# Random-feature attention: the norms placed in the spare rows of the projection's operand, one product for two, and the end of the chain moved a step

## The reference, cut to what matters

```
def _feature_map(x, rf):
    proj = jnp.einsum('bhnd,fd->bhnf', x, rf) / jnp.sqrt(jnp.float32(NUM_FEATURES))
    norm = jnp.linalg.norm(x, axis=-1, keepdims=True)
    return jnp.exp(proj - norm)
# on layernorm(x):  q' = feature_map(q), k' = feature_map(k)
kv = einsum('bhnf,bhnd->bhfd', k', v)
normalizer = einsum('bhnf,bhf->bhn', q', k'.sum(axis=2))
out = einsum('bhnf,bhfd->bhnd', q', kv) / (normalizer + 1e-06)
y = out @ w_out.T + b_out
x1 = x + layernorm(y);  what goes to the next layers is layernorm(x1)
```

## Time and profile before

| | us |
|---|---|
| median of 3 runs | 1756.01 |
| lowest and highest | 1754.92, 1756.5 |
| the profiled execution's own time | 1755.7 |
| its span | 1753.9 |
| PE busy | 1674.9 (95%) |
| DVE busy | 1446.5 (82%) |
| ACT busy | 1299.2 (74%) |
| POOL busy | 1039.0 (59%) |

### The profile page before, as it was taken

How to read it: one execution, slowest core, us unless ns; L and a number is a source line. 1 busy time by engine, 2 the same in 40 slices (tenths; PEclk the granted TensorE clock), 3 DMA queues, 4 the chain that set the end, 5 groups by cost and what they waited for, 6 DMA issues and landing times. The chain is left out here.

```text
span 1753.9 us, 54573 instructions
## 1 busy us (share of the span) xinstructions
PE 1674.9 (95%) x18245; PEld 1154.1 (66%) x18373; DVE 1446.5 (82%) x3283; ACT 1299.2 (74%) x3588; POOL 1039.0 (59%) x1015
## 2 busy tenths in 40 slices
PE   6999999979999999999989997999999999998997
PEld 4666666646777777777765664777777777775664
DVE  3777777769999999999967776899999999986996
ACT  5888888848998998989982224998998998985221
POOL 1333333337777777777763324777777777775664
PEclk9999999989999999999999999999999999999999
DMA  3211111111111111111113321111111111113443
GB/s 118 69 48 48 48 48 48 43 43 35 44 39 39 42 40 37 42 42 36 42 50 94 92 76 37 38 43 45 33 42 45 33 42 45 33 40 88 110 122 86
DMA packets 201095, 94.02 MB, mean 54 GB/s; under 512 B 82578, under 2 KB 192060, under 8 KB 201020
## 3 DMA queue, kind: packets, MB, share of 16 engines
q1 hardware_dynamic: 201020, 93.06, 20.1%
HBM read 51.00 MB, written 25.23 MB: 43 GB/s over the span
## 5 line engine op out<-in xcount | busy, mean ns | idle before, releaser
L846 ACT ACTIVATE pr<-banks,nb,rr 128x128 f32<-128x128 f32 x1024 | 456.3, 465 | 5.0 <-DVE nb L915 5.0
L747 POOL TENSOR_TENSOR rr<-ss,half_neg 128x16 f32<-128x16 f32 x128 | 374.4, 2925 | 19.0 <-POOL ss L744 17.0
L764 POOL TENSOR_TENSOR pr<-pr,rl 128x512 f32<-128x512 f32 x256 | 266.5, 1041 | 103.3 <-DVE rl L877 103.3
L885 DVE TENSOR_REDUCE ss<-sq 128x16 f32<-128x1024 f32 x128 | 156.1, 1219 | 75.4 <-ACT sq L795 61.3
L846 ACT ACTIVATION_READ_ACCUMULATOR pr<-banks,nb,rr 128x1 f32 x1024 | 216.5, 211 | 0.0
L1216 ACT ACTIVATE f_g<-banks,b_s 128x512 f32<-128x512 f32 (+1 forms) x96 | 65.9, 686 | 202.0 <-PE banks L1300 192.2
L893 DVE TENSOR_REDUCE mx<-banks 128x8 f32<-128x1024 f32 x128 | 156.0, 1219 | 9.0 <-PE banks L1022 8.3
L383 POOL TENSOR_SCALAR a_ve<-a_mv 128x2 f32<-128x2 f32 x96 | 21.4, 223 | 226.5 <-DVE a_mv L394 223.4
L755 POOL TENSOR_TENSOR krot<-ka,rr 128x512 f32<-128x512 f32 x128 | 134.4, 1050 | 22.3 <-POOL rr L747 11.7
L974 PE MATMUL banks<-ident,pr 128*128 128x128 f32 x1024 | 141.2, 281 | 5.9 <-POOL pr L764 5.9
L837 ACT COPY pT<-banks 128x512 f32<-128x512 f32 x128 | 75.1, 587 | 95.9 <-PE banks L974 95.9
(11 more groups left out here) (126 smaller groups left out, 4210.4 us busy)
## 6 DMA issues: line engine op xcount, KB each, us to landing
ve<-vt SPq DMA_DIRECT2D x128, 128.0 KB, 2.2
hs<-y_d SPq DMA_DIRECT2D x128, 64.0 KB, 2.0
yt<-y_d SPq DMA_DIRECT2D x64, 128.0 KB, 2.1
y_d<-yn SPq DMA_DIRECT2D x64, 128.0 KB, 2.0
f_h<-y_d SPq DMA_DIRECT2D x128, 64.0 KB, 2.0
f_y<-y_d SPq DMA_DIRECT2D x64, 128.0 KB, 2.2
xa<-in_L_attn_x SPq DMA_DIRECT2D x32, 128.0 KB, 2.2
xr<-in_L_attn_x SPq DMA_DIRECT2D x32, 128.0 KB, 2.3
```

The costliest lines, as they stand in the source:

```text
L747: nc.gpsimd.tensor_tensor(rr[:, r, :], ss[:, r, :], half_neg[:], ALU.pow).then_inc(T["rr"], 1)
L764: nc.gpsimd.tensor_tensor(pr[:, e], pr[:, e], rl[:, e].unsqueeze(2).broadcast_to([P, UH, P]), ALU.mult).then_inc(T[("ne", "no")[e]], 1)
L846: a = nc.scalar.activation(pr[:, e, j, :], bank[e][:, j * P:(j + 1) * P], ACT.Exp, bias=nb[:, X.t, UH * e + j:UH * e + j + 1], scale=rr[:, ...
L885: nc.vector.tensor_reduce(ss[:, 2 * X.p + X.t, :], sq[:].rearrange("p (h d) -> p h d", d=DH), AX.X, ALU.add).then_inc(T["ss"], 1)
```

## The change

The row of a head's norm moves. In each group of 32 rows the heads 0 and 1 own the rows 0 to 15, the heads 2 and 3 the rows 16 to 31; now the norms of heads 0 and 1 are put in rows 16 and 17 and those of heads 2 and 3 in rows 0 and 1. For each pair of heads one operand of 32 rows is built, which holds the pair's data in its own half and its norms in the other, and one product with `rfx` = `rfa` + `rfn` replaces the two. GpSimd multiplies the copied q and k by a column of ones and zeros, once for each pair (`qkm`), and VectorE adds the norms, multiplied by the opposite column (`xn2`). The q features need as many columns as before in one product in place of two (16 products become 8); the k features need 16 products as before, of 128 columns instead of 256. PE's product of k features and values now stands ahead of the sums of squares. The normalisation of y, x1, its statistics, its inverse deviation, its store and `a_yo` are done one step later, and `a_yo` on GpSimd.

```
 norm_rows:
-            row = 32 * g + h
+            row = 32 * g + (16 + h if h < 2 else h - 2)
+    lower = (np.arange(P) % 32 < 16).astype(np.float32)
+    return neg, np.concatenate([ones, own, np.stack([lower, 1.0 - lower], 1)], 1)
 setup_vector:
+            dve.wait_ge(set_done, 2 + 1 + 5)
+            nc.vector.tensor_tensor(rfx[:], rfa[:], rfn[:], ALU.add).then_inc(set_done, 1)
 a_sync:
             if on.last:
                 n = i - 3
+                sp.wait_ge(A["x1"], n + 1)
+                sp.dma_start(x1_d[...], a_x1[:, 1 - p]).then_inc(A[f"out{1 - p}"], 16)
                 sp.wait_ge(A["yo"], n + 1)
                 ...
-            if on.tail:   (the same store, n = i - 2)
 a_pool:
+            if on.now:
+                pool.wait_ge(A["sq"], i + 1)
+                until(pool, A["xn2"], 2 * i)
+                apart(pool)
+                for a in range(2):
+                    j = nc.gpsimd.tensor_scalar(qkm[:, a], qkT[:], hones[:, P + 4 + a:P + 5 + a], None, ALU.mult)
+                j.then_inc(A["qkm"], 1)
+            if on.last and part in (None, 1):
+                (wait yn, xr_in, out)
+                nc.gpsimd.tensor_tensor(a_x1[:, 1 - p], a_y2[:], xr[:, 1 - p], ALU.add).then_inc(A["x1"], 1)
             if on.tail: inv_std of y, i - 2
+            if on.last: inv_std of x1, i - 3
             if on.pre: inv_std of the input
+            if on.last and part in (None, 2):
+                pool.wait_ge(A["rs3"], n + 1)
+                apart(pool)
+                for t in range(TPB):
+                    j = nc.gpsimd.tensor_scalar(a_yo[:, 1 - p, t, :], a_x1[:, 1 - p, t, :], a_mv3[:, t, 0:1],
+                                                a_rs3[:, t:t + 1], ALU.subtract, ALU.mult)
+                j.then_inc(A["yo"], 1)
 a_act:
+                until(act, A["qkm"], i)        (ahead of the copy into qkT)
+                until(act, A["xn2"], 2 * i)    (ahead of the square root)
 a_pe, behind, q features:
-                    for w, src in ((rfa, qkT), (rfn, nrm)):
-                        for c in range(4):
-                            m = matmul(bank[c][:, a * N:(a + 1) * N], w[r, a * P:(a + 1) * P],
-                                       src[r, 1 - p, 0, :], start=w is rfa, stop=w is rfn)
+                    for c in range(4):
+                        m = matmul(bank[c][:, a * N:(a + 1) * N], rfx[r, a * P:(a + 1) * P],
+                                   xn2[r, 1 - p, a, 0, :], start=True, stop=True)
 a_pe, order after it: product of k features and values, sums of squares, output projection,
   transposition of the product, v projection, transposition of the input
 a_pe, now, k features:
-                pe.wait_ge(A["nrm"], i + 1)
-                for t in range(TPB):
-                    for w, src in ((rfa, qkT), (rfn, nrm)):
-                        for c in range(4):
-                            m = matmul(bank[c][:, t * N:(t + 1) * N], src[r, p, 1, t * P:(t + 1) * P],
-                                       w[r, :], start=w is rfa, stop=w is rfn)
+                for a in range(2):
+                    pe.wait_ge(A["xn2"], 2 * i + a + 1)
+                    for t in range(TPB):
+                        for c in range(4):
+                            m = matmul(bank[c][:, t * N + a * P:t * N + (a + 1) * P],
+                                       xn2[r, p, a, 1, t * P:(t + 1) * P], rfx[r, a * P:(a + 1) * P],
+                                       start=True, stop=True)
 a_dve, order after the input normalisation (a_yo is gone): normalisation of y of i - 3, copy of the
   product, bias of y of i - 2, placing in kvb, and then
+            if on.now:
+                dve.wait_ge(A["nrm"], i + 1)
+                dve.wait_ge(A["qkm"], i + 1)
+                until(dve, A["qf_ps"], i - 1)
+                for a in range(2):
+                    nc.vector.scalar_tensor_tensor(out=xn2[:, p, a].rearrange("p q n -> p (q n)"), in0=nrm[:],
+                                                   scalar=hones[:, P + 5 - a:P + 6 - a], in1=qkm[:, a],
+                                                   op0=ALU.mult, op1=ALU.add).then_inc(A["xn2"], 1)
   and the statistics of y (i - 2), of x1 (i - 3) and of the input (i + 2)
 between the stages:
   SP: the steps B+1 and B+2 of a_sync stand in slots 3 and 5 of stage T (before: 1 and 3)
   POOL, DVE: the step B+2 stands in the slots 2 and 3, in two parts (before: DVE alone, in slot 3)
```

More of the change, by code:

```diff
@@ L472, in a_act @@
                 nc.scalar.activation(a_sq[:], bank[4][:], ACT.Square)
-                nc.scalar.copy(qkT[:, p].rearrange("p a n -> p (a n)"), bank[4][:]).then_inc(A["sq"], 1)
+                until(act, A["qkm"], i)
+                nc.scalar.copy(qkT[:], bank[4][:]).then_inc(A["sq"], 1)
             if on.behind:
@@ L481, in a_act @@
                 act.wait_ge(A["ss_ps"], i + 1)
-                nc.scalar.activation(nrm[:, p].rearrange("p a n -> p (a n)"), bank[4][:], ACT.Sqrt
-                                     ).then_inc(A["nrm"], 1)
+                until(act, A["xn2"], 2 * i)
+                nc.scalar.activation(nrm[:], bank[4][:], ACT.Sqrt).then_inc(A["nrm"], 1)
                 act.wait_ge(A["v_ps"], i + 1)
@@ L545, in a_pe @@
             if on.now:
+                pe.wait_ge(A["sq"], i + 1)
+                nc.tensor.matmul(bank[4][:], hones[:, 0:P], a_sq[:], start=True, stop=True).then_inc(A["ss_ps"], 1)
+            if on.tail:
+                pe.wait_ge(A["o"], k + 1)
+                for t in range(TPB):
+                    m = nc.tensor.matmul(bank[7][:, t * P:(t + 1) * P], a_oT[:, t * P:(t + 1) * P],
+                                         wT[:, 3, :], start=True, stop=True)
+                m.then_inc(A["w_ps"], 1)
+            if on.behind:
+                pe.wait_ge(A["kvT"], n + 1)
+                for r in range(2):
+                    m = nc.tensor.transpose(bank[5][:, N + r * P:N + (r + 1) * P], a_kvT[:, r * P:(r + 1) * P],
+                                            ident[:])
+                m.then_inc(A["kv_ps"], 1)
+            if on.now:
                 if on.tail:
@@ L626, in a_dve @@
                 nc.vector.tensor_copy(a_kvT[:], bank[5][:, 0:N]).then_inc(A["kvT"], 1)
+            if on.tail and part in (None, 1):
+                dve.wait_ge(A["w_ps"], k + 1)
+                if on.last:
+                    dve.wait_ge(A["yn"], l + 1)
+                nc.vector.tensor_tensor(a_y[:], bank[7][:, 0:N].rearrange("p (t d) -> p t d", d=D),
+                                        bout[:].unsqueeze(1).broadcast_to([P, TPB, D]), ALU.add).then_inc(A["y"], 1)
+            if on.behind:
                 dve.wait_ge(A["kv_ps"], n + 1)
@@ L636, in a_dve @@
                 j.then_inc(A["kv"], 1)
-            if on.tail and part in (None, 2):
-                dve.wait_ge(A["rs2"], k + 1)
-                until(dve, A["x1"], k)
-                for t in range(TPB):
-                    j = normal(a_y2, a_y, a_mv2, a_rs2, t)
-                j.then_inc(A["yn"], 1)
+            if on.now:
+                dve.wait_ge(A["nrm"], i + 1)
[5 more added lines that the diff above has]
+                                                   op0=ALU.mult, op1=ALU.add).then_inc(A["xn2"], 1)
+            if on.tail and part in (None, 1):
+                dve.wait_ge(A["y"], k + 1)
+                until(dve, A["rs2"], k)
+                stats(dve, a_y, a_st2, a_mv2, TPB, A["st2"], 2 * (k + 1), A["mv2"])
+            if on.last and part in (None, 2):
+                dve.wait_ge(A["x1"], l + 1)
+                until(dve, A["yo"], l)
+                stats(dve, a_x1[:, 1 - p], a_st3, a_mv3, TPB, A["st3"], 2 * (l + 1), A["mv3"])
             if on.pre:
```

85 lines of the change are left out of this document (31 added, 54 removed), and 2 rows, old and new, of the table A.

## The result

The changed kernel takes 1757.64 us (median of 20 runs, 1755.09 to 1762.26), the kernel before 1755.10 (20 runs, 1753.33 to 1758.39): the ratio is 1.0016, with an interval of 1.0010 to 1.0022. The forecast was 1749.7 us and faster. The measurement says no change, or 0.1 to 0.2% slower.

The account below looks back on a forecast made before the run. PE's work, nearly level with a ring through ACT, was taken as the bound. 31 steps x (10.7 - 10.96 + 0.01) = -7.8, +1.5 at the ends, from 1755.7: 1749.4, as median 1749.7 us; range 1731 to 1766.

Parts of the forecast that it names:

- The step: One looped step of stage A, first product to next first product: from 10.96 us to 10.67, taken as 10.7 with waits.
- T: In stage A, the start of a step's first product on PE, from which the prediction counts its times.
- I take 0.80: GpSimd's mask, a `tensor_scalar` of 128x512 in stage A: 0.80 us each, between estimates of 0.77 and 1.04.
- 0.36 a half: `a_yo` on GpSimd: 0.36 us for each half, 0.7 in all.
- So the first half of `a_xn` waits for mask A, the second for mask B: VectorE in stage A takes whole-instruction turns with GpSimd's masks; without that a step would be 10.05 us.
- Rival (1): GpSimd's masks become stage A's bound: 1763 us with masks of 1.04, 1777 with 1.27; chance 0.30.
- G: Length of one GpSimd mask in stage A, forecast 0.80 us; a step was put at 9.07 + 2G.
- Rival (2): Stage A's masks and `a_xn` don't hinder each other, or masks are under 0.5: step 10.05, total 1729 us; chance 0.20.
- Rival (3): Stage A's k features stay bound by operand loads at 1.94 us: step 11.07, total 1761 us; chance 0.10.
- PE idle 1 to 2 us ahead of the k features: A sign in stage A that the forecast is right: PE idles 1 to 2 us, ended by `xn2`.
- Sum at the ends +1.5 (0 to +4): Filling and draining of stage A, including stage T's later start, together cost 1.5 us, between 0 and 4.
- I work out 0.7 later: At stage T's start, SP's `hs` loads wait for `a_yo` of batch 29 on GpSimd: 0.7 us later.

Follow-up runs that it names:

- e2: The changed kernel with GpSimd's two masks as a product of two tensors, the second a broadcast column, instead of `tensor_scalar`: 1779.13 us, ratio 1.0144 to the kernel before.
- e5: The changed kernel with the chain's end as before (`a_yo` on VectorE, y's statistics ahead of the product's copy), one product kept: 1808.17 us, ratio 1.0298.
- e9: e7 plus one wait, so that GpSimd starts x1 only when the pair `xn2` is done: 1736.76 us, ratio 0.9900 to the kernel before.
- e1: The changed kernel with two filler products on PE ahead of its wait for `xn2`: 1752.39 us, ratio 0.9990 to the kernel before.
- e8: e6 with the masks taken from GpSimd, one made by ACT's scaled copy, the other by VectorE from bank 4: 1760.99 us, ratio 1.0035 to the kernel before.
- e10: e9 without the two filler products: 1742.54 us, ratio 0.9921 to the kernel before.
- e4: The kernel before with only the chain's end moved a step later and `a_yo` on GpSimd, no masks, two products for the features: 1761.64 us, ratio 1.0043.
- e7: e6 with the `a_yo` of the last two batches on VectorE in slots 3 and 4 of stage T: 1742.14 us, ratio 0.9925 to the kernel before.
- e3: The changed kernel with SP's first `hs` loads for stage T issued ahead of its wait for `a_yo` of batch 29: 1750.27 us, ratio 0.9978 to the kernel before.
- e6: The changed kernel with both the filler of e1 and the early loads of e3: 1746.35 us, ratio 0.9948 to the kernel before.
- e11: e9 with the second half of `a_yo` left out in the looped steps, so output incomplete: 1734.06 us (one run).

## Why the prediction was wrong

**The step was right, by errors that cancel.** Forecast 10.67, measured 10.65; that the two agree is luck. The placing ends 0.52 earlier than forecast, and the pair takes 0.42 longer. Counted from T = 209.55 as in the prediction:

| | forecast | measured |
|---|---|---|
| q exponentials start | T+2.27 | T+2.27 |
| square root ends | T+6.13 | T+6.27 |
| masks start, end | T+2.6, T+4.3 | T+3.03, T+6.17 |
| `a_xn` ends | T+4.4 | T+3.79 |
| placing ends | T+6.85 | T+6.33 |
| pair `xn2` | 1.29 | 1.71 |
| pair ends (E) | T+8.15 | T+8.07 |
| E to the next T | 2.52 | 2.58 |

Two readings in the prediction were loose besides. In the earlier trace rows VectorE ends 0.34 behind GpSimd, but the forecast lets the second half of `a_xn` end 0.1 behind mask B, so that those rows would have given a step some 0.2 longer. And the 339.7 us from 15.0 to 354.7 hold a first step of 9.29 and end with the last product of the last step, not its first (353.94); the steps in the middle are 10.96 all the same.

"I take 0.80" for a mask failed (1.57), and so did "0.36 a half" for `a_yo` (0.80). The Trainium skill, "GPSIMD Engine Reference", 3.1 Elementwise, has 769 ns for a tight loop over 512 elements; this case's `tensor_scalar` over 512 takes twice that, and the measurement decides.

"So the first half of `a_xn` waits for mask A, the second for mask B" failed too. The rows it was read from the earlier trace rows had a two-tensor instruction on GpSimd, and e2 shows that these do hold VectorE up so (pair 1.42); the masks that were built do it less (1.06). The Trainium skill, "SBUF — State Buffer", Who interferes with whom, makes no such difference between GpSimd's instructions: whoever issues first has the pair of ports for the whole instruction. By that rule an `a_xn` half could wait up to 1.57, and the trace's longest is 0.817; the measurement decides.

The pair was put at 1.29. It is 1.42 alone (e5, e9), and 0.28 more because GpSimd's x1 falls on it. That the prediction names among what would make it wrong; e9 confirms it.

Rival (1), a slower kernel from G = 0.93 on, had its condition met (1.57) and yet not its result, since its price rested on the same turns (9.07 + 2 x 1.57 = 12.2 a step). Rival (2)'s "masks and `a_xn` don't get in each other's way" is nearer the mechanism, but long masks end with the square root, not ahead of it. Rival (3) is out: 1.39 for all of the k features, forecast 1.2.

**The first failed step: a term is missing, TensorE's clock.** The prediction wrote "PE idle 1 to 2 us ahead of the k features" as something to be seen and charged nothing for it. PE idles 1.48 us a step, and in six steps the granted clock fell for a part of the step from 2.4 GHz to 1.2. It took 7.2 of the 8.7 us that the steps had won in the profiled run, and by the ratios of e1 about 4.6. e1 shows the cause: with 0.82 us of filler a step, and nothing else changed, the falls are gone. The Trainium skill, "TensorE: Matmul & The Clock Gate", Part 1, says that the clock follows how busy PE has been lately; the trace of e1 agrees (1.00 again in all of stage A's middle), while e8 and e10 show that the share of busy time doesn't tell by itself which kernel has falls.

**The second failed step is "Sum at the ends +1.5 (0 to +4)".** e4 measures the moved end at 7.4 us by itself. "I work out 0.7 later" for `hs`: in e4, whose steps are those of before, the loads are issued 3.35 us later. In the changed kernel PE's wait grew from 2.65 to 6.15, 3.5 us, because PE was done earlier and `hs` was not. Stage T began at 376.08 against 375.95, so that what stage A had still won (373.3 to 369.9) was lost in that one wait. The forecast also put GpSimd's two `a_yo` inside stage T at nothing. The first six slots take 3.9 us longer than before. e7, which moves the two to VectorE, gets 4.0 us back, but they are not all of the 3.9: in e3 they stand where they did and the slots take only 0.7 longer than before, with a short wait ahead of them and a clock of 0.95 instead of 0.85. So the long wait has a price of its own behind it, and the shares are not separated.

With the filler and the early loads together (e6) the ratio is 0.9948, where the forecast, 1749.7 to 1756.01, had 0.9964.

**The sum, put together again**: steps -8.7, falls of the clock +7.2, the start and the drain -1.9 (what is left of 3.4 at PE's end of stage A), wait for `hs` +3.5, slots of stage T +3.9: +4.0 us, which is how much later the sixth slot starts. The span is 5.6 longer; the other 1.6 was not followed further, and the medians differ by 2.5.

## What to carry to other kernels

When a change takes work off TensorE and leaves it waiting in a loop, look at the granted clock of each step: here most of a saving of 0.3 us a step was undone by one step in five with a fall, and cheap products in the gap got it back. Where a pipelined stage ends, follow each moved step past the queue that starts the next stage: here a store ahead of the first load decided when it began. And a price for one engine holding up another is read for the same kind of instruction: the shorter of two equivalent ones was the dearer by 1.3% of the whole.

## What the runs showed of the hardware that was not expected

- A GpSimd `tensor_scalar` of 128x512 with a column as its scalar takes 1.57 us, a `tensor_tensor` with a broadcast column 1.04. Two halves of `a_xn` on VectorE take 0.82 (e5, e11) to 1.06 beside the first and 1.42 beside the second, 0.59 beside neither.
- A GpSimd `tensor_scalar` of 128x128 with two columns takes 0.80 us; VectorE's takes 0.34.
- VectorE's `scalar_tensor_tensor` of 128x512 takes 0.75, its addition of two tensors of that shape 0.69; beside a GpSimd addition a pair of them takes 1.71 in place of 1.42, and GpSimd's addition is not lengthened (0.72).
- The granted clock falls in a loop whose single idle times are 1.07 and 0.41 us of 10.65, in some steps and not in others that look the same. PE's busy share doesn't order the kernels: 87.1% with 0.98, 86.6% (e8) with 1.00.
